# Recurrence of a gated scan: seventeen unused products per step on PE, and two squares ahead of the sum of squares on ScalarE

## What is computed

```python
def step(h, inp):
    x_t, dt_t, B_t, C_t, xr_t = inp
    h_carrier = h.mean(axis=1)
    T = jnp.cos((c_phase(xr_t) - c_phase(h_carrier)) / 2.0) ** 2
    alpha = jnp.exp(dt_t[..., None] * A_neg)
    expo = 1.0 + (1.0 - alpha) * KAPPA * (1.0 - T[:, None, :])
    mag, ph = (c_mag(h), c_phase(h))
    cmag = jnp.minimum(jnp.exp(expo * jnp.log(mag + 1e-08)), 10.0)
    h = from_polar(cmag, ph)
    Bx = B_t[:, None, :, :] * (dt_t * x_t)[:, :, None, None]
    h = h + Bx
    h = from_polar(jnp.tanh(c_mag(h)), c_phase(h))
    y_t = jnp.einsum('bnc,bdnc->bd', C_t, h)
    return (h, y_t)
```

## Time and profile before

| | before |
|---|---|
| median of three runs | 12653.35 us |
| profiled execution | 12647.4 us |
| its span, first to last instruction | 12645.5 us |
| PE busy | 10574.1 us (84%) |
| VectorE busy | 10103.6 us (80%) |
| ScalarE busy | 8436.4 us (67%) |
| granted TensorE clock, mean | 0.756 of full speed |
| the unused products (L548) | 15872, busy 5429.8 us, mean 488 ns |

### The profile page before, as it was taken

One profiled execution on the slowest core, in us unless ns is written; L12 is line 12 of the kernel. 1 busy time (PEld: TensorE's weight loads), 2 busy tenths in 40 slices (PEclk: granted clock), 3 DMA queues, 4 the chain that ended last, 5 costly groups with the idle time before them and its releaser, 6 DMA issues. The chain is left out here.

```text
span 12645.5 us, 256282 instructions
## 1 busy us (share of the span) xinstructions
PE 10574.1 (84%) x68398; PEld 5344.3 (42%) x68414; DVE 10103.6 (80%) x56587; ACT 8436.4 (67%) x42451; POOL 94.9 (1%) x165
## 2 busy tenths in 40 slices
PE   6888888888888888888888888888888977898998
PEld 5333333333333333333333333333344546653335
DVE  5888888888888888888888888888874948868875
ACT  6777777777777777777777777777754722264666
POOL 0000000000000000000000000000000100000000
PEclk8666766766676667667666766766678988998999
DMA  2000100001000100001000100001000000011100
GB/s 57 15 15 15 21 15 15 15 18 18 15 15 15 21 15 15 15 15 21 15 15 15 22 15 15 15 15 21 15 11 12 1 24 6 7 36 45 29 24 22
DMA packets 339594, 229.62 MB, mean 18 GB/s; under 512 B 27662, under 2 KB 324184, under 8 KB 337885
## 3 DMA queue, kind: packets, MB, share of 16 engines
q1 hardware_dynamic: 338140, 213.30, 8.0%
HBM read 187.41 MB, written 25.43 MB: 17 GB/s over the span
## 5 line engine op out<-in xcount | busy, mean ns | idle before, releaser
L548 PE MATMUL scan_p_car<-scan_warm 128*128 128x448 bf16 x15872 | 5429.8, 488 | 1007.6 <-DVE scan_state_ps L674 998.6
L548 PEld LDWEIGHTS scan_p_car<-scan_warm 128*128 128x128 bf16 x15872 | 1505.7, 116 | 3689.3 <-DVE scan_state_ps L674 2101.6
L595 ACT ACTIVATE scan_act_ps<-scan_state_ps 128x64 f32<-128x64 f32 x2048 | 426.0, 208 | 1865.2 <-DVE scan_state_ps L674 1865.2
L595 ACT ACTIVATE scan_act_ps<-scan_act_ps 128x64 f32<-128x64 f32 (+1 forms) x8193 | 1610.7, 197 | 65.5
L677 DVE SCALAR_TENSOR_TENSOR scan_uw<-scan_w,scan_rsq 128x64 f32<-128x64 f32 x2048 | 461.3, 225 | 857.9 <-ACT scan_rsq L595 857.9
L536 PEld LDWEIGHTS scan_p_car<-scan_hs,scan_mean_mat 32*32 32x32 f32 x16392 | 371.4, 124 | 1811.9 <-DVE scan_hb L677 1799.2
L541 PE MATMUL scan_p_car<-scan_eps_row,ones 1*128 1x3 f32 x4102 | 1015.9, 315 | 39.1 <-DMA scan_a_log<-L_attn_a_A_log 38.9
L570 PE MATMUL scan_p_y<-scan_c_masked,scan_hb 128*64 128x4 f32 x16384 | 1030.5, 228 | 0.0
L536 PE MATMUL scan_p_car<-scan_hs,scan_mean_mat 32*32 32x2 f32 x16392 | 547.6, 191 | 564.4 <-DVE scan_hb L677 542.0
L674 DVE TENSOR_TENSOR scan_c<-scan_V,scan_power_ps 128x64 f32<-128x64 f32 x4096 | 722.3, 217 | 242.3 <-ACT scan_power_ps L595 18.5
L541 PEld LDWEIGHTS scan_p_car<-scan_eps_row,ones 1*128 1x128 f32 x4102 | 837.9, 254 | 72.0 <-DMA scan_a_log<-L_attn_a_A_log 39.3
(11 more groups left out here) (453 smaller groups left out, 18338.8 us busy)
## 6 DMA issues: line engine op xcount, KB each, us to landing
scan_step_in<-scan_scratch SPq DMA_DIRECT2D x520, 256.0 KB, 6.2
qk_scratch<-qkv_parts SPq DMA_DIRECT2D x32, 384.0 KB, 2.5
attn_qT<-qk_scratch SPq DMA_DIRECT2D x192, 64.0 KB, 2.2
attn_kT<-qk_scratch SPq DMA_DIRECT2D x192, 64.0 KB, 2.2
scan_scratch<-prep_dts SPq DMA_DIRECT2D x32, 256.0 KB, 2.1
x<-L_attn_a_x SPq DMA_DIRECT2D x1, 4096.0 KB
out<-x SPq DMA_DIRECT2D x1, 4096.0 KB
filter_in_taps<-c_kT SPq DMA_DIRECT2D x1, 2048.0 KB
```

Source lines behind the costliest of these rows:

```text
L548: nc.tensor.matmul(p_car[slot][:, 64:512], warm[:, 0:P], warm[:, 64:512], start=True, stop=True)
L595: nc.scalar.activation(dst, src, func, **kw).then_inc(counts[par]["act"], 1)
```

## The change

- keep_busy is called at other places and seventeen times in a step, in every step: four products after r2, four after E, then the carrier, epsilon and the output products as before, and nine after dot. In the last step of a chunk, which had none, there are nine too. The products after r2 and E go to the other slot of p_car.
- On VectorE sq1 and na go. sq0 stays. r2 adds sq0 and sq1, n2 adds nq and sq1.
- On ScalarE two Squares come, between alpha (with the table or masked copy behind it) and l: nq = (w0 + eps)^2, written to SBUF, which waits for w0, and sq1 = w1^2, written to PSUM (power_ps), which waits for w1. r2 on VectorE now waits for sq1.
- The lists of names change with this: 22 to 20 operations on VectorE, 18 to 20 on ScalarE. PE waits once, ahead of its loop, for nsq and dot of the initial state.

```diff
--- before.py
+++ after.py
@@ -404,8 +404,8 @@
 
 
 
-DVE_STEP = ["c0", "c1", "w0", "w1", "sq0", "sq1", "na", "r2", "n2", "bx0", "bx1", "uw0", "uw1", "h0", "h1", "nh", "hp", "Vm", "dot", "dl", "s", "V"]
-ACT_STEP = ["al", "l", "M", "ln2", "E", "rsq", "L1", "R", "th2", "l2", "mag", "nsq", "lm", "lnn", "lnh", "rs", "ru", "cm"]
+DVE_STEP = ["c0", "c1", "w0", "w1", "sq0", "r2", "n2", "bx0", "bx1", "uw0", "uw1", "h0", "h1", "nh", "hp", "Vm", "dot", "dl", "s", "V"]
+ACT_STEP = ["al", "nq", "sq1", "l", "M", "ln2", "E", "rsq", "L1", "R", "th2", "l2", "mag", "nsq", "lm", "lnn", "lnh", "rs", "ru", "cm"]
 PE_STEP = ["carrier", "y"]
 STEPS = {"dve": (DVE_STEP, "h0"), "act": (ACT_STEP, "l2"), "pe": (PE_STEP, "carrier")}
 
@@ -446,13 +446,13 @@
         a_neg, a_log, a_pos = ph.sb("a_neg", [P, 1]), ph.sb("a_log", [P, 1]), ph.sb("a_pos", [P, 1])
         alpha = ph.sb("alpha", [P, 2, J])
         hb = ph.sb("hb", [P, 2, 3, J])
-        c, w, sq, uw, bx, Vm, V = (ph.sb(n, [P, 2, J]) for n in ("c", "w", "sq", "uw", "bx", "Vm", "V"))
-        na, rsq, R, th2, mag, ru = (ph.sb(n, [P, J]) for n in ("na", "rsq", "R", "th2", "mag", "ru"))
+        c, w, uw, bx, Vm, V = (ph.sb(n, [P, 2, J]) for n in ("c", "w", "uw", "bx", "Vm", "V"))
+        sq0, nq, rsq, R, th2, mag, ru = (ph.sb(n, [P, J]) for n in ("sq0", "nq", "rsq", "R", "th2", "mag", "ru"))
         act_ps, state_ps, norm_ps, power_ps = (ph.ps(n, [P, 512]) for n in ("act_ps", "state_ps", "norm_ps", "power_ps"))
         lr, E2, ln2, M, L1, l2, lnh = (act_ps[:, q * J:(q + 1) * J] for q in range(7))
         r2, dl = (state_ps[:, q * J:(q + 1) * J] for q in range(2))
         n2, nh = (norm_ps[:, q * J:(q + 1) * J] for q in range(2))
-        lm, cm = (power_ps[:, q * J:(q + 1) * J] for q in range(2))
+        lm, cm, sq1 = (power_ps[:, q * J:(q + 1) * J] for q in range(3))
         hs, products = ph.sb("hs", [P, 2]), ph.sb("products", [P, 2])
         squares, nsq, lnn = act_ps[:, 448:451], act_ps[:, 456:457], act_ps[:, 464:465]
         dot, s_, rs = (ph.sb(n, [P, 1]) for n in ("dot", "s", "rs"))
@@ -554,6 +554,8 @@
                 after(pe, "pe", "carrier", 1, CS - 1)
                 pe.sem_inc(counts[1]["pe"], 1)
                 epsilon(0)
+                after(pe, "act", "nsq", 1, CS - 1)
+                after(pe, "dve", "dot", 1, CS - 1)
                 with nc.Fori(0, NCH // CHUNKS, engines=[mybir.EngineType.PE], hint_back_edge=True) as i:
                     for q in range(CHUNKS):
                         par, n = q % 2, i * CHUNKS + q
@@ -562,6 +564,10 @@
                         pe.sem_inc(taken, 1)
                         for k in range(CS):
                             slot = k % 2
+                            after(pe, "dve", "r2", par, k)
+                            keep_busy(1 - slot, 4)
+                            after(pe, "act", "E", par, k)
+                            keep_busy(1 - slot, 4)
                             after(pe, "dve", "h1", par, k)
                             carrier(par, slot)
                             epsilon(1 - slot)
@@ -572,13 +578,8 @@
                                                             start=(comp == 0), stop=(comp == 1))
                             last.then_inc(counts[par]["pe"], 1)
                             leave(pe, k)
-                            if k < CS - 1:
-                                after(pe, "dve", "dot", par, k)
-                                keep_busy(slot, 4)
-                                after(pe, "dve", "r2", par, k + 1)
-                                keep_busy(slot, 3)
-                                after(pe, "act", "E", par, k + 1)
-                                keep_busy(slot, 1)
+                            after(pe, "dve", "dot", par, k)
+                            keep_busy(slot, 9)
                 epsilon(0, start=False)
 
             @block.scalar
@@ -646,12 +647,16 @@
                                 copy_table(1 - par, (n + 1) * CS)
                             if TAB_STEP < k <= TAB_STEP + MASKS:
                                 mask_table(1 - par, n + 1, k - TAB_STEP - 1)
+                            after(act, "dve", "w0", par, k)
+                            op(par, nq[:, :], w[:, 0, :], ACT.Square, bias=EPS_PHASE)
+                            after(act, "dve", "w1", par, k)
+                            op(par, sq1[:, :], w[:, 1, :], ACT.Square)
                             after(act, "dve", "r2", par, k)
                             op(par, lr[:, :], r2[:, :], ACT.Ln, bias=EPS_MAG)
                             after(act, "act", "l", par, k)
                             op(par, M[:, :], lr[:, :], ACT.Exp, scale=0.5)
                             after(act, "dve", "n2", par, k)
-                            op(par, ln2[:, :], n2[:, :], ACT.Ln, scale=SHIFT * SHIFT, bias=SHIFT * SHIFT * (EPS_PHASE * EPS_PHASE + 1e-24))
+                            op(par, ln2[:, :], n2[:, :], ACT.Ln, scale=SHIFT * SHIFT, bias=SHIFT * SHIFT * 1e-24)
                             after(act, "act", "M", par, k)
                             op(par, E2[:, :], M[:, :], ACT.Exp, scale=-2.0)
                             after(act, "act", "ln2", par, k)
@@ -742,15 +747,12 @@
                             for comp in range(2):
                                 after(dve, "dve", f"c{comp}", par, k)
                                 tt(sem, w[:, comp, :], c[:, comp, :], bx[:, comp, :], ALU.add)
-                            for comp in range(2):
-                                after(dve, "dve", f"w{comp}", par, k)
-                                tt(sem, sq[:, comp, :], w[:, comp, :], w[:, comp, :], ALU.mult)
+                            after(dve, "dve", "w0", par, k)
+                            tt(sem, sq0[:, :], w[:, 0, :], w[:, 0, :], ALU.mult)
                             after(dve, "dve", "sq0", par, k)
-                            stt(sem, na[:, :], w[:, 0, :], 2 * EPS_PHASE, sq[:, 0, :], ALU.mult, ALU.add)
-                            after(dve, "dve", "sq1", par, k)
-                            tt(sem, r2[:, :], sq[:, 0, :], sq[:, 1, :], ALU.add)
-                            after(dve, "dve", "na", par, k)
-                            tt(sem, n2[:, :], na[:, :], sq[:, 1, :], ALU.add)
+                            after(dve, "act", "sq1", par, k)
+                            tt(sem, r2[:, :], sq0[:, :], sq1[:, :], ALU.add)
+                            tt(sem, n2[:, :], nq[:, :], sq1[:, :], ALU.add)
                             if k == CS - 1:
                                 dve.wait_ge(dma_in[nxt], (i * (CHUNKS // 2) + (q + 1) // 2 + 1) * (DMAS * 16))
                                 dve.wait_ge(tab_in, n + 2)
```

## The result

| | before | after |
|---|---|---|
| median | 12653.35 us | 12705.97 us (five runs, 12699.08 to 12714.66) |
| ratio to before | | 1.0042, 95% interval 1.0029 to 1.0055 |
| profiled execution, its span | 12645.5 us | 12704.1 us |
| PE / VectorE / ScalarE busy | 84 / 80 / 67% | 94 / 76 / 72% |
| granted clock, mean | 0.756 | 0.975 |

The change makes the kernel 53 us slower. I had forecast 86 us off, 12567 us, with 12520 to 12625 us as the range: the time lies outside it, and on the side of slower.

The account below looks back on a forecast made before the run. The recurrence was taken as bound by 2048 times one chain through all three engines; 55 us off for the clock plus 31 for the squares made 86 off the 12653.35 us median, 12567 us, range 12520 to 12625.

Parts of the forecast that it names:

- What bounds the kernel, and the difference between the two clocks: Recurrence: one chain through three engines, 4.453 us a step; 4.40 at clock 1.00, 4.44 at 0.50, differing from carrier's load to square.
- Part 1: TensorE's clock in the recurrence: seventeen products hold 1.00 instead of 0.70, gaining 55 us (bounds 49 and 61).
- Part 2: PE's queue: seventeen products fit at 2.4 GHz at no cost, with 0.12 us to spare ahead of the carrier's load.
- carrier held up: Rival: products close ahead of the carrier cost it the clock's gain, leaving only the squares, 12622 us; chance 0.08.
- Part 3: Squares moved from VectorE to ScalarE: r2 0.66 us after first w, gain 0.015 us a step, 31 us in all.
- r2 starts some 0.035 later: Hand-off from ScalarE's sq1 to VectorE's r2: sq1 ends 0.624 us after w0 starts, r2 starts at 0.66.
- squares in the way: Rival: ScalarE holds sq1 until nq is complete, +140 us, 12793 us; chance 0.03 full, 0.05 mild (no change).
- The 0.14 I took from the row: ScalarE: the next instruction behind one reading SBUF starts 0.14 us later, so sq1 starts at 0.388 us, behind nq at 0.248.
- The irregular delays: Recurrence: the remaining 0.029 us a step, some 60 us in all, which may move by 15 us to either side.

## Why the prediction was wrong

- *What bounds the kernel, and the difference between the two clocks:* right. The step is a chain through three engines, and all that was gained or lost showed as its length.
- *Part 1, the clock stays at 2.4 GHz:* right, 1.00 throughout. Forecast 55 us, measured 60 with the products alone, just within the bounds of 49 and 61.
- *Part 2, seventeen products fit at no cost:* right in the result, wrong in the margin. The spacing of products was taken for the time until the carrier's load can start; the room is 0.02 us, not 0.12. My rival "carrier held up" was nearer than I thought.
- *Part 3, the squares:* the step that failed. Forecast a gain of 0.015 us, measured a loss of 0.05. The end of sq1 fits, by two errors that cancel (0.42 + 0.21 us after w0 against 0.388 + 0.236). The failed term is the last one, "r2 starts some 0.035 later". It measured 0.101. The prediction's row for such a hand-off is l behind r2, 0.03 us, an instruction with only one wait. The diff shows two waits ahead of r2 with the late one written last; the kernel before has them the other way round at every place on the chain, and only nh, off the chain, has them like this. I didn't ask which of two waits would be on the instruction. With the order turned, 12558 us came out for a forecast of 12567.
- *The rival "squares in the way":* it had the point from which the sign turns right, r2 later by over 0.027 us, and the wrong mechanism. It was to come from ScalarE holding sq1 back until nq is done; sq1 starts 0.16 us behind nq, which is done after 0.26. The 0.14 I took from the row was 0.02 short. That row's first activation writes to PSUM and nq to SBUF, but this is not it: with sq1 first, writing to PSUM, nq still starts 0.16 us behind. What else differs (the row's second activation has one column, reads PSUM and waits for nsq) no run tells apart. By the Trainium skill, "VectorE: DVE Perf Modes", section on the TRN2 errata, I had an estimate of 240 ns for such an activation; read as a spacing it is refused by this trace too, with 0.16 us between two activations that both read SBUF.
- *The irregular delays:* the mean step is longer than the typical step (the median of the steps wholly at one clock, mixed by the clock) by 63 us in all before and 64 after, so they did not move. Their cause was not tried.
- *The range:* it was built from the sizes of known terms and had no case for a hand-off at three times its price, though the change adds one on the chain of every step. Such a wait deserves a bound of its own.

The sum after the fact: 60 us off for the products and their clock, measured alone. Against that kernel r2 starts 0.049 us later in a step (100 us), and from r2 to l it is 0.264 instead of 0.256 us (16 us more). That makes 56 us slower, where 53 were measured. With the waits turned, r2 starts 0.022 us earlier than with the products alone and the same link is 0.007 longer: 31 us off, where the times differ by 29. So the 12558 us that came so near to the forecast of 12567 are in part luck: the clock gave 5 us more than forecast, and the squares, forecast at 31 us, gave 29 by a larger gain at r2 and a loss behind it that the prediction did not have.

## What to carry to other kernels

When an instruction waits for two semaphores, look at which wait it carries and which becomes an instruction of its own: in this kernel the one written last does, and if that is the one that comes late it costs 0.06 to 0.07 us each time. Write the late one first, and expect the same where waits pile up because the instructions between them were removed. Filler products that hold TensorE's clock are worth only what the clock gives to the few products on the chain (0.044 us of 4.4 here), so count first whether they can ever stand ahead of those, at the slow clock too.

## What the runs showed of the hardware that I had not expected

- A satisfied wait in an instruction of its own, ahead of the waiting instruction, costs nothing seen: c0, s and V, which have one, start 0.03 us after what they wait for, as uw0 does, which has none. A late one costs 0.07 us on VectorE (gap 0.10 against 0.03) and 0.06 us on PE (carrier's load 0.12 against 0.05 us after the read-out).
- The carrier's small float32 weight load starts no sooner than 0.28 us after the start of a full bf16 product of 448 columns at 2.4 GHz, while another such product starts after 0.19.
- An idle time of 3.5 us on PE did not delay its next load: it started 0.06 us after its release, as behind a busy PE.
- The first activation after idle time has a record about 0.02 us longer than the same one behind another (nq 0.257 against 0.239 us, sq1 0.228 against 0.210).
